# Fused feed-forward kernel: the half tile's last eviction and the down projection's adapter sums placed between the first groups' products, operands loaded where memory comes free

## The reference

```python
def _L0_cond_ref(hidden_states, W, b, coeff, mask):
    output = jnp.einsum('bsi,oi->bso', hidden_states, W) + b
    sign = (2 * mask - 1).astype(hidden_states.dtype)
    diff = jnp.einsum('bsi,bio->bso', hidden_states, sign)
    return output + diff * coeff[:, None, None]
...
def lora_add(base, inp, A, B):
    Ab = A[layer_idx][lora_indices]
    Bb = B[layer_idx][lora_indices]
    t = jnp.einsum('bri,bni->bnr', Ab, inp)
    return base + jnp.einsum('bor,bnr->bno', Bb, t) * SCALE
gate = lora_add(jnp.einsum('bnh,fh->bnf', x, W_gate), x, A_gate, B_gate)
up = lora_add(jnp.einsum('bnh,fh->bnf', x, W_up), x, A_up, B_up)
act = jax.nn.silu(gate) * up
down = lora_add(jnp.einsum('bnf,hf->bnh', act, W_down), act, A_down, B_down)
...
x = x + _L0_cond_ref(x, L0_cond_W, L0_cond_b, condB_coeff, mask)
x = x + _L1_cond_ref(x, ...)
```

## Time and profile before

| | |
|---|---|
| median of 3 runs | 1676.89 us (1675.64 to 1679.54) |
| profiled execution | 1675.9 us, its span 1674.2 us |
| PE busy | 94% of the span |
| DVE busy | 75% |
| ACT busy | 48% |
| mean granted clock of TensorE | 0.979 of full speed |

### The profile page before, as it was taken

One profiled execution on the slowest core, in us unless ns is written; L12 is line 12 of the kernel. 1 busy time (PEld: TensorE's weight loads), 2 busy tenths in 40 slices (PEclk: granted clock), 3 DMA queues, 4 the chain that ended last, 5 costly groups with the idle time before them and its releaser, 6 DMA issues.

```text
span 1674.2 us, 22931 instructions
## 1 busy us (share of the span) xinstructions
PE 1576.1 (94%) x7502; PEld 1319.6 (79%) x7502; DVE 1247.3 (75%) x2168; ACT 798.9 (48%) x1466; POOL 331.9 (20%) x629
## 2 busy tenths in 40 slices
PE   6999958999999999978999779999999999899999
PEld 5999946888888888867888558888888888677887
DVE  7998767666666666678888776666666666788886
ACT  7998644444444444433333344444444444433332
POOL 0101021222222222232410011222222222502210
PEclk9999969999999999999999889999999999999999
DMA  8988572444444444593973643444444444958763
GB/s 329 346 294 300 174 259 66 148 148 148 148 148 149 148 148 148 197 364 117 370 273 91 208 132 123 144 143 143 148 148 148 148 148 143 346 181 277 251 211 117
DMA packets 135813, 321.03 MB, mean 192 GB/s; under 512 B 19344, under 2 KB 42000, under 8 KB 135696
## 3 DMA queue, kind: packets, MB, share of 16 engines
q0 software_dynamic: 55072, 175.81, 31.8%
q1 hardware_dynamic: 76016, 135.37, 24.5%
q10 hardware_dynamic: 4608, 8.39, 1.3%
HBM read 229.32 MB, written 90.18 MB: 191 GB/s over the span
## 4 chain that ended last, share of the span: by engine, by line
PE 84%; DVE 8%; DMA 3%; issue 2%; ACT 1%; SPq 1%; POOL 0%; DVEq 0%; ACTq 0%; POOLq 0%
PE ps L1286 57%; PE ps L1282 25%; PE ps L1388 2%; DMA fx<-x_scratch 2%; DVE lo L935 2%; DVE acc L938 1%; DVE op_b L935 1%; DVE fx L935 1%; DMA m_raw<-in_mask 0%; DVE raw L935 0%; DMA x_in<-in_x 0%; PE ps L1367 0%; DMA x_scratch<-x_out 0%; DVE fx L938 0%; DVE xs L935 0%
## 5 line engine op out<-in xcount | busy, mean ns | idle before, releaser
L1286 PE MATMUL ps<-op_b,hi 128*128 128x512 f32 x1696 | 526.6, 392 | 15.2 <-ACT ps L641 7.5
L935 DVE TENSOR_TENSOR lo<-raw,hi 128x512 fp32r<-128x512 f32 (+2 forms) x646 | 338.3, 531 | 134.2 <-ACT hi L641 131.6
L641 ACT ACTIVATE hi<-raw 128x512 fp32r<-128x512 f32 (+1 forms) x598 | 308.9, 519 | 244.5 <-PE ps L1286 205.9
L1286 PEld LDWEIGHTS ps<-op_b,hi 128*128 128x128 f32 x1696 | 320.1, 189 | 85.5 <-ACT ps L641 8.6
L1286 PE MATMUL ps<-op_b,lo 128*128 128x512 f32 x848 | 332.6, 392 | 0.0
L1286 PE MATMUL ps<-op_d,hi 128*128 128x512 f32 x800 | 250.1, 394 | 21.1 <-DVE acc L938 12.5
L1282 PE MATMUL ps<-op_b,hi 128*128 128x512 f32 x720 | 228.4, 399 | 10.2 <-DVE op_b L935 10.2
L938 DVE TENSOR_TENSOR acc<-acc,ps 128x512 f32<-128x512 f32 x272 | 184.9, 685 | 59.7 <-PE ps L1286 56.3
L530 POOL DMA_DIRECT2D operand_scratch<-ot x140 | 75.5, 540 | 664.3 <-DVE ot L935 629.4
L1286 PEld LDWEIGHTS ps<-op_d,hi 128*128 128x128 f32 x800 | 150.9, 190 | 57.4 <-DVE acc L938 15.4
L1286 PEld LDWEIGHTS ps<-op_b,lo 128*128 128x128 f32 x848 | 160.5, 189 | 34.1
(11 more groups left out here) (123 smaller groups left out, 2202.9 us busy)
## 6 DMA issues: line engine op xcount, KB each, us to landing
operand_scratch<-ot POOLq DMA_DIRECT2D x140, 512.0 KB, 3.9
op_d<-operand_scratch POOLq DMA_DIRECT2D x140, 512.0 KB, 12.3
raw<-in_wgu SPq DMA_DIRECT2D x168, 256.0 KB, 4.2
m_raw<-in_mask SPq DMA_DIRECT2D x64, 512.0 KB, 5.7
raw<-in_wd SPq DMA_DIRECT2D x160, 128.0 KB, 4.2
fx<-x_scratch SPq DMA_DIRECT2D x64, 256.0 KB, 3.6
b_in<-in_b_gu POOLq DMA_DIRECT2D x264, 32.0 KB, 2.3
w_in<-in_w SPq DMA_DIRECT2D x16, 512.0 KB, 5.5
```

Of the source, the lines that this page charges most:

```text
L641: return nc.scalar.activation(o, i, ACT.Copy)
L935: return nc.vector.tensor_tensor(o, a, b, ALU.subtract)
L1286: return mm(dst, weight, v, start=False, stop=stop, skip_group_check=True)
```

## The change

The half tile's second half is taken out of `evict`: its product, its high copies and its low part come after p1 (behind the seed copy) and after p5 of the first down group. The adapter sums are cut in four steps (`low`, `sum`, `hi`, `ready`), which stand behind p5, p3, p7 and p4 of group 1 for the first half and of group 2 for the second. The product `("td", s, PAIRS)` moves from behind p3 to behind p2 of group 0. `opd_at` gets another order of places, so that p1 and p5 of segment 0 can be loaded when p5 of the last pair is done, p6 and p3 when its p7 is done, p7 and p2 when its p4 is done; in segment 1 the late ones are p7 and p2 instead of p1 and p5.

```diff
@@ -31,6 +31,8 @@
 PRODUCTS = ["p1", "p5", "p6", "p3", "p7", "p2", "p4"]
 FIRST_PRODUCTS = ["p1", "p2", "p5", "p6", "p3", "p7", "p4"]
 ADDED = ["p5", "p6", "p3", "p7", "p2", "p4"]
+T_DOWN_AT = {(hp, u): (hp - 1, step) for hp in (1, 2)
+             for u, step in (("p5", "low"), ("p3", "sum"), ("p7", "hi"), ("p4", "ready"))}
@@ -38,6 +40,7 @@
 MOVING = {"p1": "b11", "p5": "t1", "p6": "t2", "p3": "b22", "p7": "t3", "p2": "b21", "p4": "t4",
           "q1": "b11", "q2": "b21", "q3": "b22", "q4": "t2"}
 STORED = {MOVING[u]: i for i, u in enumerate(PRODUCTS)}
+OPERAND_AT = ["t4", "b11", "t1", "t2", "b22", "t3", "b21"]
@@ -62,10 +65,10 @@
         order += [("g", s, PAIRS, u) for u in FUSED[2:]]
         for seg in range(SEGS):
             for hp in range(HP):
-                order += [("d", s, seg, hp, u) for u in PRODUCTS[:4]]
+                order += [("d", s, seg, hp, u) for u in PRODUCTS[:6]]
                 if seg == 0 and hp == 0:
                     order += [("td", s, PAIRS)]
-                order += [("d", s, seg, hp, u) for u in PRODUCTS[4:]]
+                order += [("d", s, seg, hp, u) for u in PRODUCTS[6:]]
@@ -258,7 +261,7 @@
 
         def opd_at(seg, name, kp, low):
 
-            return ((((seg + 1) % 2) * 7 + 6 - STORED[name]) * SEGK + kp) * 2 + low
+            return ((((seg + 1) % 2) * 7 + OPERAND_AT.index(name)) * SEGK + kp) * 2 + low
@@ -591,6 +594,11 @@
                 load_b_gu(adapter, 1)
                 for kp in range(KP):
                     for name in KP_ENTRIES[1:]:
+                        if kp == KP - 1 and name == "t2":
+
+                            pool.wait_ge(pe_done, done["g", s, PAIRS - 1, "p5"])
+                            load_operand(s, 0, "p1")
+                            load_operand(s, 0, "p5")
@@ -599,28 +607,29 @@
 
                 pool.wait_ge(ot_l, ot_index[s, KP - 1, "t4"] + 1)
                 load_acc(s, 1)
-                pool.wait_ge(pe_done, done["g", s, PAIRS - 1, "p4"])
-                for u in PRODUCTS[:2]:
-                    load_operand(s, 0, u)
+                pool.wait_ge(pe_done, done["g", s, PAIRS - 1, "p7"])
+                load_operand(s, 0, "p6")
+                load_operand(s, 0, "p3")
 
                 for i in range(OT_RING):
                     pool.wait_ge(ot_stored[i], 16 * stores_upto(s)[i])
                 load_acc(s, 0)
-                for u in PRODUCTS[2:6]:
-                    load_operand(s, 0, u)
+                pool.wait_ge(pe_done, done["g", s, PAIRS - 1, "p4"])
+                load_operand(s, 0, "p7")
+                load_operand(s, 0, "p2")
                 pool.wait_ge(pe_done, done["g", s, PAIRS, "q4"])
-                load_operand(s, 0, PRODUCTS[6])
+                load_operand(s, 0, "p4")
 
                 pool.wait_ge(a21_l, HALVES * (s + 1))
                 for h in range(2, HT):
                     load_acc(s, h)
                 load_b_down(adapter)
-                for u in PRODUCTS[2:]:
+                for u in ("p1", "p5", "p6", "p3", "p4"):
                     load_operand(s, 1, u)
 
                 pool.wait_ge(lo_ready, at["l", s, HT - 1] + 1)
-                for u in PRODUCTS[:2]:
-                    load_operand(s, 1, u)
+                load_operand(s, 1, "p7")
+                load_operand(s, 1, "p2")
@@ -776,18 +785,19 @@
                     act.wait_ge(d_added, (g - 2) * len(ADDED) + ADDED.index("p2") + 1)
                 copy(ps[3 * (g % 2) + 2][:, :], ps[3 * (g % 2)][:, :]).then_inc(d_seeded, 1)
 
-            def form_t_down(s):
+            def t_down_low(s, half):
+                n = HALVES * s + half
                 act.wait_ge(pe_done, done["td", s, PAIRS])
-                for half in range(HALVES):
-                    n = HALVES * s + half
-                    if n:
-                        act.wait_ge(td_ready, 2 * n)
-                    for b in range(2):
-                        r, cols = 2 * DR * b, slice(b * S, (b + 1) * S)
-                        nc.scalar.activation(td_w[r:r + DR, 0, cols], ps[6 + half][r + DR:r + 2 * DR, cols], ACT.Copy,
-                                             scale=LORA_SCALE).then_inc(td_low, 1)
-                    act.wait_ge(td_sum, 2 * (n + 1))
-                    copy(td_h[:, :], td_w[0:DR, 1, :]).then_inc(td_hi, 1)
+                if n:
+                    act.wait_ge(td_ready, 2 * n)
+                for b in range(2):
+                    r, cols = 2 * DR * b, slice(b * S, (b + 1) * S)
+                    nc.scalar.activation(td_w[r:r + DR, 0, cols], ps[6 + half][r + DR:r + 2 * DR, cols], ACT.Copy,
+                                         scale=LORA_SCALE).then_inc(td_low, 1)
+
+            def t_down_hi(s, half):
+                act.wait_ge(td_sum, 2 * (HALVES * s + half + 1))
+                copy(td_h[:, :], td_w[0:DR, 1, :]).then_inc(td_hi, 1)
@@ -844,11 +854,15 @@
                     gate, silu = ((g1, u2), (g2, p5c))[half]
                     act.wait_ge(c_made, c_count(s, f, ("c11", "c12")[half]))
                     nc.scalar.activation(silu[HALF:P, :], gate[0:HALF, :], ACT.Silu).then_inc(silu_made, 1)
-                    act.wait_ge(a_made, a_count(s, f, half))
-                    copy(act21[0:HALF, half * N:(half + 1) * N], a32[0:HALF, 0, :])
-                    copy(act_t[0:HALF, half * N:(half + 1) * N], a32[0:HALF, 0, :]).then_inc(a21_h, 1)
                     if u == "q2":
+                        half_tile_hi(s, 0)
                         lora_a(("td", s, PAIRS))
+
+            def half_tile_hi(s, half):
+                act.wait_ge(a_made, a_count(s, PAIRS, half))
+                cols = slice(half * N, (half + 1) * N)
+                copy(act21[0:HALF, cols], a32[0:HALF, 0, :])
+                copy(act_t[0:HALF, cols], a32[0:HALF, 0, :]).then_inc(a21_h, 1)
@@ -901,6 +915,8 @@
                     evict(key)
                 elif key[0] == "d" and key[4] == "p1":
                     seed_down(key)
+                if key[0] == "d" and key[2:] == (0, 0, "p1"):
+                    half_tile_hi(key[1], 1)
@@ -917,8 +933,12 @@
                     lora_b(s, 0)
                 if key[0] == "g" and key[2:] == (0, "p5"):
                     form_t_gu(s)
-                if key[0] == "d" and key[2:] == (0, 0, "p7"):
-                    form_t_down(key[1])
+                if key[0] == "d" and key[2] == 0 and key[3:] in T_DOWN_AT:
+                    half, step = T_DOWN_AT[key[3:]]
+                    if step == "low":
+                        t_down_low(key[1], half)
+                    elif step == "hi":
+                        t_down_hi(key[1], half)
@@ -1080,24 +1100,26 @@
                         dve.wait_ge(t_top, 2 * m + i + 1) if r == 0 else dve.wait_ge(t_hi, 2 * m + 2)
                         sub(dst[2 * R2:3 * R2, :], t[r:r + R2, :], dst[r:r + R2, :]).then_inc(t_ready, 1)
 
-            def form_t_down(s):
...
+            def t_down_sum(s, half):
+                n = HALVES * s + half
+                dve.wait_ge(td_low, 2 * (n + 1))
+                for b in range(2):
+                    r, cols = 2 * DR * b, slice(b * S, (b + 1) * S)
+                    nc.vector.scalar_tensor_tensor(
+                        out=td_w[0:DR, 1, cols], in0=ps[6 + half][r:r + DR, cols], scalar=LORA_SCALE,
+                        in1=td_w[r:r + DR, 0, cols], op0=ALU.mult, op1=ALU.add).then_inc(td_sum, 1)
+                dve.wait_ge(td_sum, 2 * (n + 1))
+                nc.vector.tensor_scalar(td_w[0:DR, 0, :], td_w[0:DR, 1, :], pick[:, 0:1], None, ALU.mult
+                                        ).then_inc(td_pick, 1)
+
+            def t_down_ready(s, half):
+                n = HALVES * s + half
+                dve.wait_ge(td_pick, n + 1)
+                dve.wait_ge(td_hi, n + 1)
+                for r in (HALF, HALF + DR):
+                    nc.vector.scalar_tensor_tensor(
+                        out=act_t[r:r + DR, half * N:(half + 1) * N], in0=td_h[:, :], scalar=pick[:, 1:2],
+                        in1=td_w[0:DR, 0, :], op0=ALU.mult, op1=ALU.add).then_inc(td_ready, 1)
@@ -1154,19 +1176,26 @@
                     lora_b(s, f + 1)
                 if u in ("q2", "q4"):
                     half = int(u == "q4")
-                    gate, silu, first, second = ((g1, u2, p1c, z_ps), (g2, p5c, p1c, y_ps))[half]
+                    gate, first, second = ((g1, p1c, z_ps), (g2, p1c, y_ps))[half]
                     dve.wait_ge(pe_done, done[key])
                     dve.wait_ge(copied, copy_count(s, f, "p1"))
                     add(gate[:, :], first[:, :], second[:, :]).then_inc(c_made, 1)
-                    dve.wait_ge(c_made, c_count(s, f, ("c11", "c12")[half]))
-                    dve.wait_ge(silu_made, silu_count(s, f, half))
-                    mult(a32[0:HALF, 0, :], silu[HALF:P, :], gate[HALF:P, :]).then_inc(a_made, 1)
-                    dve.wait_ge(a_made, a_count(s, f, half))
-                    dve.wait_ge(a21_h, HALVES * s + half + 1)
```

(50 more changed lines are left out.)

## The result

| | before | changed |
|---|---|---|
| median of the runs | 1677.43 us (1675.64 to 1679.54, 4 runs) | 1666.45 us (1664.12 to 1666.76, 4 runs) |
| ratio to before | | 0.9932, 95% interval 0.9916 to 0.9947 |
| profiled execution | 1675.9 us, span 1674.2 | 1666.3 us, span 1664.6 |

The kernel became 11 us faster. The forecast was 1662.9 with a range of 1656 to 1670: the time lies inside, 3.6 us above the forecast, and within 0.1 us of the lower end of rival (B), to which 20% had been given.

A forecast was written before the change was run, and what follows sets the result against it. TensorE (PE), busy 94% of the span, was taken as the bound; stalls won at the down projection, 6.95 us in block 0 and 7.1 in block 1, took 1675.9 to 1661.9, plus 1.0 for the median: 1662.9, range 1656 to 1670.

The forecast's parts named there:

- (B): Rival: clock falls in group 0 too, 1.8 us each time, 3.6 or 7.2 in all, 1666.5 to 1670.1; 20%.
- (A): Case that the forecast holds, with a gain of 12 to 16 us; 55%.
- part 1: Group 0: half tile after the seed copy; p6's 2.08 us go, p3 still late; group 0 loses 2.9 us.
- so p3 still loses 2.7 us: Group 0: PE resumes at p3 at 718.8 where 716.14 was due, the weight tile being behind ACT's half-tile copies.
- Group 0 loses 2.9: Total loss forecast for group 0 after the change, ending at 724.9; before, it lost 4.45 us.
- part 2: Adapter sums in steps: groups 1 and 2 lose 0.7 and 1.4 us, at p4, then p3 and p4.
- does not fit: Groups 1 and 2: DVE's 7.86 us plus 2.9 of sums, 10.8, exceed a clean group's 9.52 us.
- part 3: Early operand loads: PE waits for no load, the 0.56 us of p4 go; segment 1 priced at nothing.
- (E): Rival: accumulator row 3 lands late, from 14.5 us on decisive; 2.4 us lost per block, 1681.8; 6%.
- The 0.56 us of p4: Group 0: p4's stall for a DMA load, counted as going with the early operand loads.
- (D): Rival: bias rows too late for ACT's copy ahead of the left tiles, gain given back, 1676.9; 7%.
- (C): Rival: DVE and ACT keep up, p3 waits less or only one 0.7 us stall comes; likelier 1658; 10%.

The follow-up runs named there:

- filled: Changed kernel plus nine matmuls with unused results ahead of p3's wait in group 0; 1665.8 us, ratio 0.9924.
- changed_again: The changed kernel, unchanged, measured again; 1665.2 us, ratio 0.9920 to the kernel before.
- operands_only: Kernel before with only the operands' new places and loading order; 1677.9 us, ratio 0.9999.
- steps_only: Kernel before with only the adapter sums cut in steps, half tile and operand loads as before; 1665.1 us, ratio 0.9927.
- order_groups: order_dve with DVE adding before it prepares weights in groups 1 and 2 too; 1659.2 us, ratio 0.9898.
- steps_operands: Changed kernel with the half tile back in one piece ahead of the seed copy; 1664.1 us, ratio 0.9910.
- order_old_loads: order_dve with the operands' places and loads of the kernel before; 1666.0 us, ratio 0.9917.
- order_dve: Changed kernel with the half tile one product later and DVE adding before it prepares weights in group 0; 1659.0 us, ratio 0.9885.
- order_again: Same kernel as order_dve, measured a second time; 1660.5 us, ratio 0.9898.

## Why the prediction was right, point by point

The time lies in the range because the range was drawn to hold (B) as well. Of the rivals it is (B) that came, in both blocks, at 1.6 us each where 1.8 was put; (A), the forecast itself with its gain of 12 to 16 us, was missed by the measured 11.0.

- **p6 and the seed** (part 1): right. The seed copy starts at +2.27 (forecast +2.13), p6 at +2.89 instead of the old +4.73.
- **p3** (part 1): the start was right (+6.84, forecast +6.76), and so was its cause, the weight tile behind ACT's copies. The step that failed is the price of the wait: "so p3 still loses 2.7 us". It counts the idle time and the restart alone, while the units that follow at half speed cost 1.6 us more. The sum "Group 0 loses 2.9" is really 4.5 (14.47-9.98). I had set this term as rival (B) at 20%, because one wait of 2.60 us in the earlier trace rows had been followed by full speed. filled and changed_again show that it is no matter of chance for this wait: six of six fell, and neither of the two that were filled. Nor does it hang on the wait's length alone, by which (B) was weighed: the wait of 2.60 us, to which it was compared, belongs to another place, where ten more of 2.34 to 2.62 us in the other profiles kept the full clock as well (last section). Where the wait was split in two, as before, the clock stayed up in seven of eight groups and fell in one (operands_only, block 1). What was mis-sized is this one term, 1.6 us twice, 3.2 of the 3.6 us between forecast and result.
- **Adapter sums** (part 2): right to 0.13 us. Groups 1 and 2 were put at 10.22 and 10.92 us and took 10.21 and 11.05, with waits at p4, p3, p4 as named; steps_only shows that this is the whole gain. That the rest is DVE's load, as "does not fit" had it, is shown in part: order_groups moves the waits and leaves their sum, with DVE busy for 19.2 us where PE has 19.0 us of work.
- **Operands** (part 3): no wait for a load in the changed kernel, as forecast, and row 3 of the accumulators (issued at 722.9) landed in 5.1 us, where 4.5 had been put, in time; the rival (E) with its 14.5 us is far off. That segment 1's part is worth nothing was right too (operands_only). The 0.56 us of p4 were counted as a gain, and operands_only shows them in group 0 of block 0, but group 1 took them back: its p6 starts 19.37 us after group 0 does, with the early loads or without them; the seed for it stands behind the block of sums, which is not early because PE is. With the sums in steps they are a gain indeed: block 0 takes 35.66 us in steps_only and 35.10 in steps_operands.
- **(D)** did not come: ACT's copy of the bias rows (752.27) follows the seed at once, and groups 3 to the end of the left tiles take 33.72 us, as before 33.73. The chain of DVE moved with PE.
- **(C)** did not come, nor would it have from DVE: its operations took the very durations of the earlier trace rows.
- Not in the sum: the first group of segment 1, 1.1 us of gain in this profile, by the clock (last section). That is luck: twelve of the 24 such groups had it, twelve had not.

## What to carry to other kernels

A wait is priced by its idle time, its restart and the clock behind it. In group 0 two waits of 1.8 and 1.4 us with work between them cost less (13.83 us) than one of 2.3 (14.47 us), so joining waits can eat what a shorter chain brings; the length of a wait alone does not tell which it will be. When a step is moved off a critical copy, look at what the same two engines do next. Here, letting DVE evict before it prepares, together with the half tile one product later, was worth 3 us a block, where the move alone had cost 0.6. A part that gives nothing by itself (the early loads) may be what the next gain needs, so undo it again on the better kernel before it is dropped.

## What the runs showed of the hardware

The granted clock fell behind each of six waits of 2.28 or 2.29 us in group 0, which came after 1.7 us of work and another gap too short to be listed as a wait; the wait of 1.43 us there in steps_only was followed by full clock. It also fell behind two shorter ones, of 1.81 us (operands_only, block 1; seven like it were followed by full clock) and of 1.28 us (order_old_loads, block 1). At the place of the earlier trace rows in gate/up, which comes once in each block, longer waits did less harm: eleven of 2.34 to 2.62 us were followed by a granted clock of 1.00, and only the other thirteen, of 3.00 to 3.16 us, by one of 0.61 to 0.67. The kernel before has one of each:

```profile
266.89:271.00 4.11, 3.26 (x13) 2.37 (x13) 3.57 (x6) 2.25 (x4) 0.00 (x0) 1.00 0.00 0
995.59:1000.00 4.41, 4.41 (x12) 3.58 (x13) 3.22 (x5) 1.61 (x3) 0.00 (x0) 0.61 0.00 0
```

The wait of 2.17 to 2.19 us at the start of segment 1 went both ways: in these profiles its group took 11.15 to 11.25 us or 10.66 to 10.70, twelve times each. It did so in the same kernel in one block the one and in the other block the other (steps_only 10.68 and 11.23, operands_only 11.24 and 10.68), and in two profiles of the same kernel (order_dve 10.70 and 10.69, order_again 11.15 and 11.20). The granted clock of the 5 us behind it was 1.00 in the one case and 0.66 or 0.67 in the other. In steps_operands the first pair after it took 0.70 in block 0 and 1.15 in block 1:

```profile
781.78 0.70 PE L1311 MATMUL ps<-op_d,hi 128*128 128x512 f32 x2 [2.19 <-issue]
...
1504.95 1.15 PE L1311 MATMUL ps<-op_d,hi 128*128 128x512 f32 x2 [2.18 <-issue]
```

So a wait of one length may or may not cost the clock. Why 2.29 us do so each time at one place, 2.2 us half of the times at another, and 2.6 us never at a third, is left open; no run varied the work ahead of these waits. The Trainium skill, TensorE: Matmul & The Clock Gate, Part 1, says that the watching does not start with the kernel, so that the point of a change varies from run to run. The start of segment 1 agrees with it (order_dve against order_again), the six waits of group 0 do not show it.
